# Windowed attention in a four-layer network: context times both weight matrices first, four tiles of scores in one PSUM bank, another order of work in each group

## The reference, cut to what matters

```
attn_start = jnp.maximum(p_t - WINDOW, 0.0)                  # WINDOW = 16
attn_end = jnp.minimum(p_t + WINDOW, src_end)
mask = (idx[None, :] < attn_start[:, None]) | (idx[None, :] > attn_end[:, None])
score = jnp.einsum('nqh,hk,nlk->nql', decoder_h_t, W_a, encoder_outputs)
score = jnp.where(mask[:, None, :], -1000000000.0, score)
align = jax.nn.softmax(score, axis=2)
gauss = jnp.exp(-(idx[None, :] - p_t[:, None]) ** 2 / DEV_POW)
align = align * gauss[:, None, :]
context = jnp.einsum('nql,nlh->nqh', align, encoder_outputs)
cat = jnp.concatenate([context, decoder_h_t], axis=2)
return jnp.tanh(cat @ W_c.T)
```

## Time and profile before

| what | value |
|---|---|
| median of 3 runs | 3458.16 us (3453.02 to 3458.41) |
| the profiled execution's own time | 3459.26 us |
| its span | 3457.5 us |
| PE busy over the span | 3138.2 us (91%) |
| DVE, ACT, POOL busy | 2359.8 (68%), 1109.2 (32%), 983.6 us (28%) |
| mean granted TensorE clock | 0.959 |

### The profile page before, as it was taken

One profiled execution on the slowest core, in us unless ns is written; L12 is line 12 of the kernel. 1 busy time (PEld: TensorE's weight loads), 2 busy tenths in 40 slices (PEclk: granted clock), 3 DMA queues, 4 the chain that ended last, 5 costly groups with the idle time before them and its releaser, 6 DMA issues. The chain is left out here.

```text
span 3457.5 us, 67521 instructions
## 1 busy us (share of the span) xinstructions
PE 3138.2 (91%) x27670; PEld 2384.3 (69%) x27670; DVE 2359.8 (68%) x6222; ACT 1109.2 (32%) x1989; POOL 983.6 (28%) x1010
## 2 busy tenths in 40 slices
PE   5999999899599947777899999999999987999999
PEld 4776766566377724466688888888888875777444
DVE  5777355100477758654788888888888883778666
ACT  3444211122245548643322222222222212454100
POOL 2342000233234440000244344354354352342000
PEclk9999999999799979988899999999999998999999
DMA  3100220243410000112000000000000002100000
GB/s 125 39 26 2 71 70 19 58 117 81 127 35 30 2 10 1 55 49 92 31 1 2 1 1 2 1 1 2 1 2 1 1 1 76 38 26 2 13 19 19
DMA packets 81169, 108.24 MB, mean 31 GB/s; under 512 B 11744, under 2 KB 62176, under 8 KB 80480
## 3 DMA queue, kind: packets, MB, share of 16 engines
q1 hardware_dynamic: 74720, 95.40, 8.5%
q0 software_dynamic: 6144, 8.52, 1.3%
HBM read 87.00 MB, written 16.91 MB: 30 GB/s over the span
## 5 line engine op out<-in xcount | busy, mean ns | idle before, releaser
L2069 POOL TENSOR_TENSOR pk_hisig<-pk_hihot,pk_sigs 128x512 f16<-128x512 f16 x512 | 520.4, 1044 | 668.3 <-DVE pk_hihot L2276 667.4
L2130 PE MATMUL pk_ps<-pk_nt,ew_downT 128*128 128x128 f32 x4096 | 515.5, 279 | 0.0
L2130 PEld LDWEIGHTS pk_ps<-pk_nt,ew_downT 128*128 128x128 f32 x4096 | 479.7, 192 | 15.3 <-issue 15.3
L2171 PE MATMUL pk_ps<-ew_up,pk_act_h 128*128 128x256 f32 x2048 | 450.4, 381 | 0.9 <-DVE pk_act_h L2264 0.9
L2171 PEld LDWEIGHTS pk_ps<-ew_up,pk_act_h 128*128 128x128 f32 x2048 | 388.8, 191 | 53.1 <-issue 1.0
L2077 ACT ACTIVATE pk_act_h<-pk_ps 128x512 f32<-128x512 f32 x256 | 152.9, 597 | 542.2 <-PE pk_ps L2130 542.2
L2277 DVE TENSOR_TENSOR pk_lohot<-pk_iota_h,pk_ps 128x1024 f16<-128x1024 f16 x256 | 310.6, 1213 | 0.0
L579 DVE RECIPROCAL a_rden<-a_ps_o 128x256 f32<-128x256 f32 x96 | 168.3, 1753 | 159.4 <-PE a_ps_o L464 159.4
L568 DVE TENSOR_REDUCE a_mx<-a_ps_s 128x8 f32<-128x1024 f32 x192 | 226.0, 1219 | 54.8 <-PE a_ps_s L438 54.5
L273 ACT ACTIVATE a_pT<-a_ps_t 128x512 f32<-128x512 f32 x384 | 208.9, 599 | 144.2 <-PE a_ps_t L447 144.0
L2450 PE MATMUL mo_ps<-mw_we,mo_xnT 128*128 128x512 f32 x512 | 225.6, 599 | 0.0
(11 more groups left out here) (353 smaller groups left out, 5395.4 us busy)
## 6 DMA issues: line engine op xcount, KB each, us to landing
ro_w<-in_L_W SPq DMA_DIRECT2D x16, 1024.0 KB, 7.1
a_ctx_t<-in_ctxT SPq DMA_DIRECT2D x24, 512.0 KB, 3.8
a_tau<-in_tau SPq DMA_DIRECT2D x24, 256.0 KB, 4.1
a_delta<-in_delta SPq DMA_DIRECT2D x24, 256.0 KB, 4.4
X<-in_x SPq DMA_DIRECT2D x4, 1024.0 KB, 9.4
row_dram<-sh_row SPq DMA_DIRECT2D x8, 512.0 KB, 3.0
sum_dram<-sh_new SPq DMA_DIRECT2D x8, 512.0 KB, 2.9
X<-sum_dram SPq DMA_DIRECT2D x4, 1024.0 KB, 9.5
```

The source lines that it names most:

```text
L2069: ins = pool.tensor_tensor(hisig[:, buf, n, :, :, :], hi, sig2.broadcast_to([P, TP, 2, ECH]), ALU.mult)
L2130: ins = pe.matmul(hid.bank(f"h{c}")[:, j * P:(j + 1) * P], downT[:, k, e * P:(e + 1) * P], nt[:, s, k, :], start=(k == 0), stop=(k == KC - 1))
L2171: ins = pe.matmul(tail.bank("y")[:, 0:D], act_h[:, s, c, :], up[:, c, :], start=(c == 0), stop=(c == ECH - 1))
```

## The change

The mathematics is regrouped and the order of the work rewritten, in this block alone.
- Score: before (h W_a) ctx, now h (W_a ctx). PE `products` computes keysT = W_a ctx, four matmuls 512 wide (waT is W_a laid out transposed), and ACT copies it out. There is no `queries` any more.
- Output: before (al ctx) W_c1 + h W_c2, now al (ctx W_c1) + h W_c2. `products` also computes vals = ctx W_c1, eight matmuls 256 wide, two tiles to a bank. `sums` then needs three matmuls of 256 a tile instead of four, and the context product (eight of 128) and its copy are gone. The context in row layout (`ctx_r`) is no longer loaded; ctx_t has two buffers.
- The scores of four tiles go into one bank, and DVE reads them with one instruction. So do the four transposes of al, which ACT copies with one instruction. Tanh takes two tiles at a time.
- The eight banks are four rings of two: cp (products), xt (transposed xn), sa (scores and transposed al), ys (sums).
- Order: products and columns are computed two groups ahead. The diff below is cut to the new functions and orders; `maxima` and `weights` together hold the same DVE instructions as `weights` before, but for the one read of the scores. Of the removed lines only the two rings are shown; the others stand in the listing above.

```diff
-        first = Ring(f"{tag}_first", sem, banks[0:4], ["xt0", "xt1", "a0", "a1"] + [f"sc{u}" for u in range(G)])
-        second = Ring(f"{tag}_second", sem, banks[4:8], [f"{n}{u}" for n in ("al", "cx", "y") for u in range(G)])
+        cp = Ring(f"{tag}_cp", sem, banks[0:2], ["k0", "k1", "v0", "v1"])
+        xt = Ring(f"{tag}_xt", sem, banks[2:4], ["xt0", "xt1"])
+        sa = Ring(f"{tag}_sa", sem, banks[4:6], ["sc", "al"])
+        ys = Ring(f"{tag}_ys", sem, banks[6:8], ["y0", "y1"])
...
@@ sync @@
+            for g in range(2, GROUPS):
+                cp.wait_full(sp, g - 2, "v1")
+                sp.dma_start(ctx_t[:, g % 2, :, :], ctxT_v[:, :, g * GT:(g + 1) * GT]).then_inc(ctx_loaded[g % 2], 16)
...
@@ scalar @@
+            def products(g):
+                if g >= 1:
+                    sa.wait_full(act, g - 1, "sc")
+                for c in range(KC):
+                    cp.wait_full(act, g, f"k{c}")
+                    cp.take(act.activation(keysT[:, c, :], cp.bank(f"k{c}")[:, :], ACT.Copy), f"k{c}")
+                if g >= 2:
+                    ys.wait_full(act, g - 2, "y1")
+                for n in range(2):
+                    cp.wait_full(act, g, f"v{n}")
+                    cp.take(act.activation(vals[:, g % 2, 2 * n:2 * n + 2, :].rearrange("p a n -> p (a n)"),
+                                           cp.bank(f"v{n}")[:, :], ACT.Copy), f"v{n}")
...
+            products(0)
+            columns(0)
...
+            distances(0)
+            exps(0)
+            products(1)
+            columns(1)
+            distances(1)
+            for g in range(GROUPS):
+                turned_weights(g)
+                if g + 1 < GROUPS:
+                    exps(g + 1)
+                tanhs(g)
+                if g + 2 < GROUPS:
+                    products(g + 2)
+                    columns(g + 2)
+                    distances(g + 2)
...
@@ tensor @@
+            def products(g):
+                s = g % 2
+                pe.wait_ge(ctx_loaded[s], g // 2 * 16 + 16)
+                for c in range(KC):
+                    cp.claim(pe, g, f"k{c}")
+                    for k in range(KC):
+                        ins = pe.matmul(cp.bank(f"k{c}")[:, :], waT[:, k, c * P:(c + 1) * P], ctx_t[:, s, k, :],
+                                        start=(k == 0), stop=(k == KC - 1))
+                    cp.filled(ins)
+                for n in range(2):
+                    cp.claim(pe, g, f"v{n}")
+                    for u in (2 * n, 2 * n + 1):
+                        for k in range(KC):
+                            ins = pe.matmul(cp.bank(f"v{n}")[:, u % 2 * D:(u % 2 + 1) * D],
+                                            ctx_t[:, s, k, u * P:(u + 1) * P], wc[:, k, :], start=(k == 0),
+                                            stop=(k == KC - 1))
+                    cp.filled(ins)
...
+            def scores(g):
+                for n in range(2):
+                    xt.wait_taken(pe, g, f"xt{n}")
+                for c in range(KC):
+                    cp.wait_taken(pe, g, f"k{c}")
+                sa.claim(pe, g, "sc")
+                for u in range(G):
+                    at = slice(u * P, (u + 1) * P)
+                    for k in range(KC):
+                        ins = pe.matmul(sa.bank("sc")[:, at], xnT[:, g % 2, k, at], keysT[:, k, at], start=(k == 0),
+                                        stop=(k == KC - 1))
+                sa.filled(ins)
+
+            def turned_weights(g):
+                sa.claim(pe, g, "al")
+                for u in range(G):
+                    pe.wait_ge(al_ready, g * G + u + 1)
+                    ins = pe.transpose(sa.bank("al")[:, u * P:(u + 1) * P], al[:, u, :], ident[:, :])
+                sa.filled(ins)
+
+            def sums(g):
+                s = g % 2
+                for n in range(2):
+                    ys.claim(pe, g, f"y{n}")
+                    if n == 0:
+                        sa.wait_taken(pe, g, "al")
+                    cp.wait_taken(pe, g, f"v{n}")
+                    for u in (2 * n, 2 * n + 1):
+                        dst = ys.bank(f"y{n}")[:, u % 2 * D:(u % 2 + 1) * D]
+                        for k in range(KC):
+                            pe.matmul(dst, xnT[:, s, k, u * P:(u + 1) * P], wc[:, KC + k, :], start=(k == 0), stop=False)
+                        ins = pe.matmul(dst, alT[:, u, :], vals[:, s, u, :], start=False, stop=True)
+                    ys.filled(ins)
+
+            w.wait(pe)
+            products(0)
+            columns(0)
+            scores(0)
+            products(1)
+            columns(1)
+            for g in range(GROUPS):
+                turned_weights(g)
+                if g + 1 < GROUPS:
+                    scores(g + 1)
+                sums(g)
+                if g + 2 < GROUPS:
+                    products(g + 2)
+                    columns(g + 2)
...
@@ vector @@
+            def maxima(g):
+                link = Tally(weight_link, g, WEIGHT_LINKS)
+                dve.wait_ge(mask_link, 3 * g + 3)
+                sa.wait_full(dve, g, "sc")
+                sa.take(dve.tensor_tensor(sc[:, :, :].rearrange("p a n -> p (a n)"), sa.bank("sc")[:, :],
+                                          inside[:, :, :].rearrange("p a n -> p (a n)"), ALU.mult), "sc")
+                sa.wait_taken(dve, g, "sc")
+                link.inc(dve.tensor_tensor(sc[:, :, :], sc[:, :, :], low[:, :, :], ALU.add))
...
+            masks(0)
+            norm(1)
+            link = maxima(0)
+            masks(1)
+            weights(0, link)
+            for g in range(GROUPS):
+                if g + 2 < GROUPS:
+                    norm(g + 2)
+                if g + 1 < GROUPS:
+                    link = maxima(g + 1)
+                if g + 2 < GROUPS:
+                    masks(g + 2)
+                if g + 1 < GROUPS:
+                    weights(g + 1, link)
+                rows(g)
```

More of the change, by code:

```diff
@@ L1655, in distances @@
[L1655 to L1665, removed]
-                    first.take(act.activation(aT[:, k, :], first.bank(f"a{k}")[:, :], ACT.Copy), f"a{k}")
@@ L1699, in _ @@
         @block.tensor
         def _(pe):
-            for r in (first, second):
+            for r in (cp, xt, sa, ys):
                 r.start_empty(pe)
-            w.wait(pe)
+            def products(g):
[15 more added lines that the diff above has]
+                    cp.filled(ins)
@@ L1719, in queries @@
                 for c in range(KC):
-                    first.claim(pe, g, f"a{c}")
+                    cp.wait_taken(pe, g, f"k{c}")
+                sa.claim(pe, g, "sc")
+                for u in range(G):
+                    at = slice(u * P, (u + 1) * P)
                     for k in range(KC):
-                        ins = pe.matmul(first.bank(f"a{c}")[:, :], wa[:, k, c * P:(c + 1) * P], xnT[:, s, k, :],
-                                        start=(k == 0), stop=(k == KC - 1))
-                    first.filled(ins)
@@ L1737, in turn @@
-            def turn(g, s, more):
-                for u in range(G):
-                    second.claim(pe, g, f"al{u}")
-                    pe.wait_ge(al_ready, g * G + u + 1)
-                    second.filled(pe.transpose(second.bank(f"al{u}")[:, 0:P], al[:, u, :], ident[:, :]))
-                if more:
-                    columns(g + 1)
-                pe.wait_ge(ctx_r_loaded, g * 16 + 16)
-                for u in range(G):
-                    second.claim(pe, g, f"cx{u}")
-                    second.wait_taken(pe, g, f"al{u}")
-                    for c in range(KC):
-                        ins = pe.matmul(second.bank(f"cx{u}")[:, c * P:(c + 1) * P], ctx_r[:, u, c * P:(c + 1) * P],
-                                        alT[:, u, :], start=True, stop=True)
-                    second.filled(ins)
-                if more:
-                    queries(g + 1, 1 - s)
-                for u in range(G):
-                    second.claim(pe, g, f"y{u}")
-                    second.wait_taken(pe, g, f"cx{u}")
-                    for k in range(2 * KC):
-                        lhs = cxT[:, u, k, :] if k < KC else xnT[:, s, k - KC, u * P:(u + 1) * P]
-                        ins = pe.matmul(second.bank(f"y{u}")[:, 0:D], lhs, wc[:, k, :], start=(k == 0),
-                                        stop=(k == 2 * KC - 1))
-                    second.filled(ins)
-                    if u == 1 and more:
-                        scores(g + 1)
@@ L1780, in _ @@
[L1780 to L1781 removed]
             def norm(g):
[L1784 to L1786 removed]
+                if g >= 1:
+                    xt.wait_full(dve, g - 1, "xt1")
                 for u in range(G):
```

189 lines of the change are left out of this document (66 added, 123 removed).

## The result

The changed kernel takes 3410.1 us (median of 4 runs, 3406.37 to 3412.33), against 3457.35 of the kernel before (4 runs, 3453.02 to 3458.41): 0.9863 of the time, 95% interval 0.9851 to 0.9875, or 47 us less. The forecast was 3416, 42 less.

A forecast was written before the change was run, and what follows sets the result against it. PE's waits, mainly 4.5 us a turn for al behind ACT's late exponentials, and the clock they lower set the block's time. Start +7.5, middle -45.7, end -3.9 gave -42.1, so 3416 us; own case 3410 to 3422, wider 3405 to 3432.

The forecast's parts named there:

- turn 7: Seventh turn, which holds no products or columns: 9.0 us and 0.1 for al(7).
- tail: From the last al transposes to the block's last DVE instruction: 9.7 us against 13.6, so -3.9.
- PE's work is unchanged by the regrouping: PE's matmul work per group: 6.9 us off, 6.9 on; all depends on the waits and the clock.
- al is in time with 6 us to spare: Scores-to-al chain in a turn: al complete at 10 us, wanted at 16.8; the 4.51 us wait goes.
- Two pauses a turn, for xnT and for alT: PE waits for ACT's copies: 0.8 us before the scores, 0.75 before the sums, making a turn 16.8 us.
- The clock holds at the seam: At each turn's seam the two short gaps lose no clock: cost taken as 0, from the row of `bit_ffn`.
- The first rival: Clock falls at each seam: seven turns lose 1.8 to 2.7 us each, 3429 to 3435; chance 0.12.
- Transposes don't hold the clock up: Reason for the clock falling at the seam: 1650:1660, transposes only with gaps, was granted 0.53.
- The start costs 7.5: Block's start: first al transposes at 1462.7 instead of 1455.25, with 4 us at half rate and 1.7 lost to ACT's order.
- The seam costs nothing: Rival at the turn's seam: copies overlap better, seven times 1.5 us less, 3406; chance 0.07.
- slower: Rival: clock low for most of the block; at half rate throughout, seven turns +57, about 3500; chance 0.04.
- nothing gained: Rival: al stays late, needing 6 us more in its chain or product copies blocking ACT; al or ACT late 0.05.

The follow-up runs named there:

- three moves in the order: Kernel before, old algebra: PE's next-group scores one tile earlier, exponentials behind the first tanh, DVE's next weights ahead of the first row; 3409.0 us.
- the two order experiments: Changed kernel with gauss instructions moved behind the copy of alT, 3407.2 us; changed kernel with columns ahead of products on PE and ACT, 3409.4 us.
- the experiments with longer pauses: Changed kernel with two, three or four idle-making ACT instructions added each turn, before the sums or (two, three) the scores; 3415.6 to 3436.1 us.
- the best kernel: Changed kernel with columns ahead of products, also at the start, gauss behind alT, and the alT wait behind the first tile's xnT matmuls; 3396.6 us.

## Why the prediction was right, point by point

| step | predicted | measured |
|---|---|---|
| first al later, from the block's start | +7.5 | +8.1 (26.7 against 18.6) |
| turns 1 to 6 | 16.8 each | 16.32 each |
| turn 7 | 9.1 | 8.57 |
| first to eighth al | -45.7 | -49.1 (106.5 against 155.6) |
| tail | -3.9 | -4.1 (9.6 against 13.6) |
| block | -42.1 | -45.1 |

- *PE's work is unchanged by the regrouping, and everything hangs on the waits and the clock*: right. The old algebra reached the same time with three moves in the order.
- *al is in time with 6 us to spare*: right, 7.0.
- *Two pauses a turn, for xnT and for alT*: right in place and cause, as the two order experiments show; mis-sized. I counted 0.8 and 0.75, from single durations of 0.60 us a copy; by starts they are 0.57 and 0.51. Start to start ACT's queued instructions overlap: both xnT copies take 1.08 us together where I had 1.20, and from the first xnT copy to the end of alT it takes 3.4 where I had 3.75. PE's added time a turn is 1.1 us (16.32 against the 15.17 without pauses), not 1.6. Seven times 0.5 is the 3.4 us that the middle came out shorter.
- *The clock holds at the seam*: right in each of the turns. The row of `bit_ffn` with its 1.25 us pauses was the right one to go by; in these kernels it held up to 1.7 us of standing and no longer always at 2.4, not far off. The first rival did not come true here, but it is what happened in the experiments with longer pauses, at 1.1 to 1.7 us a fall where I had put 1.8 to 2.7. The Trainium skill ("TensorE: Matmul & The Clock Gate", section "A second HAM failure mode: psum-queue depth-cycling") says that frequent short idling between groups of matmuls can make the clock swing. Two pauses of 0.5 us a turn did not do it here; it is seen with the 4.5 us of the kernel before and where pauses were made longer.
- *Transposes don't hold the clock up*, the rival's reason: no support at this seam, and I misread the row that I took for it. Its 0.53 is the end of a longer story, on PE in the kernel before (columns as the earlier trace rows):

```profile
1627.00:1640.00 13.00, 13.00 (x63) 0.50 0.99 386
1640.00:1647.00 7.00, 5.74 (x26) 0.50 1.09 350
...
1648.00:1649.00 1.00, 1.00 (x8) 1.00 1.09 349
```

From 1640.13 on PE did nothing but transposes, with gaps, and behind 7 us of them the clock rose to 1.00, from about 1647.1 to 1650.5; ahead of them it had stayed at 0.50 through 13 us of float32 matmuls 64 columns wide, without a gap in PE's records. So the 0.53 does not show that transposes count for nothing; the prediction says that it agrees with that, and it doesn't. What decides in this stretch is open.

- *The start costs 7.5*: 8.1. The time at half rate was 5.7 us and not 4, 0.8 us more lost; ACT's order cost 1.23 us and not 1.7. The row that I went by would have said so: I counted the old start's 5.3 us from 1440.4, a time of the new kernel, but the old one's PE restarted at 1439.85, 5.9 us before the clock came back.
- *The seam costs nothing, slower, nothing gained*: none of them. The mean clock was 0.98. In the rival with the clock low throughout, the 57 us more in seven turns would give about 3515, not the 3500 that I wrote.
- The forecast of 42 us was 5 short of the 47 measured: 3 of them are the block's, by the middle; the other 2 lie outside the block and are within the spread of the runs.

## What to carry to other kernels

When an engine idles at the same place in each turn, follow the chain back to the instruction that was ready and not started. Here ACT, an engine busy 44% of the block, had the exponentials queued behind work that nobody needed so soon; two moved calls gave 32 of the 47 us, and issuing the scores one tile earlier, with the exponentials and DVE's part moved to match, the rest, with no new algebra. The new factoring leaves the matmul columns as they are, and the old one reached its time; ask first what the order gives. Whether the old factoring could also reach the 3396.6 us of the best kernel was not tried. In the order written anew, put the copies that the next matmuls wait for ahead of those that have time: 6.5 us more here, and 13.5 with the block's start and the wait for alT reordered too.

## What the runs showed of the hardware

- The clock could fall and hold in turns of one kernel with the same pause (2.4 us: 18.2 and 19.9 us mixed). Two kernels that stand at other places (3.2 us in one piece ahead of al, 3.0 before the sums) settled at the same turn of 20.47 to 20.48 us; why, no run here shows.
- At the block's start PE ran at 1.2 GHz for 2.9 us behind 4.2 us of idle time in one kernel, and for 3.7 to 5.8 us behind 5.3 to 5.8 in ten others that start alike among themselves.
- PE's records can be without a gap and the clock still at 1.2 GHz: 13 us of float32 matmuls 64 columns wide ran at a granted clock of 0.50, and it rose to 1.00 only in the stretch of transposes with gaps behind them.
- Queued ACT instructions of 0.60 us start 0.5 us apart: two copies take 1.08.
